# Short diagonal tiles of an attention pass: two or four heads in one PSUM bank and one exponential, with the written order rearranged

## The reference, cut to what matters

```python
scores = jnp.einsum('bhqd,bhkd->bhqk', Q, K)
causal = jnp.tril(jnp.ones((n, n), dtype=jnp.float32))
mask = (1.0 - causal) * -100000.0
attn = jax.nn.softmax((scores + mask) / math.sqrt(d), axis=-1)
out = jnp.einsum('bhqk,bhkd->bhqd', attn, V)
```

## Time and profile before

| | |
|---|---|
| median of 3 runs | 942.92 us (940.74 to 944.81) |
| the profiled execution, its own time | 941.0 us |
| its span, first to last instruction | 939.0 us |
| mean granted TensorE clock | 0.99 |
| PE busy | 900.1 us, 96% |
| VectorE (DVE) busy | 784.4 us, 84% |
| ScalarE (ACT) busy | 597.2 us, 64% |
| GpSimd (POOL) busy | 376.2 us, 40% |

### The profile page before, as it was taken

The page is one execution under the profiler, slowest core; times in us unless marked ns, Lnnn a source line. Parts: engine busy times, 40 slices in busy tenths (PEclk is TensorE's granted clock), DMA queues, the critical chain, the costliest instruction groups (busy, mean ns, idle before and its releaser), DMA issues.

```text
span 939.0 us, 17696 instructions
## 1 busy us (share of the span) xinstructions
PE 900.1 (96%) x5646; PEld 535.8 (57%) x5646; DVE 784.4 (84%) x2529; ACT 597.2 (64%) x1365; POOL 376.2 (40%) x526
## 2 busy tenths in 40 slices
PE   6788999899999999999999999999999999999996
PEld 5633355356665756456555656466565755555675
DVE  6889997998789799989889898998889998894543
ACT  3235676567766675776767675776767675776734
POOL 3713413323545335433364235534354224422434
PEclk9879999999999999999999999999999999999999
DMA  5311101200101011110021101110011011000000
GB/s 188 65 36 49 37 26 35 77 8 4 49 30 64 2 36 37 64 38 26 10 67 50 35 10 38 52 37 28 27 61 35 13 44 37 19 19 13 1 12 23
DMA packets 45980, 35.19 MB, mean 37 GB/s; under 512 B 10816, under 2 KB 44608, under 8 KB 45760
## 3 DMA queue, kind: packets, MB, share of 16 engines
q1 hardware_dynamic: 43680, 31.97, 10.7%
q10 hardware_dynamic: 2208, 2.10, 0.8%
HBM read 4.28 MB, written 4.19 MB: 9 GB/s over the span
## 4 chain that ended last, share of the span: by engine, by line
PE 84%; DVE 10%; ACT 2%; issue 2%; ACTq 1%; DMA 0%; SPq 0%; POOL 0%; POOLq 0%; DVEq 0%
PE bank_w L594 14%; PE bank_p L576 13%; PE bank_s L546 13%; PE bank_f L682 6%; PE bank_f L684 6%; PE bank_f L683 6%; PE bank_f L480 3%; PE bank_f L482 3%; PE bank_f L481 3%; PE bank_m L648 3%; DVE bank_s L784 3%; DVE mx_far L780 3%; PE bank_m L622 2%; PE bank_m L612 1%; PE bank_m L632 1%
## 5 line engine op out<-in xcount | busy, mean ns | idle before, releaser
L1051 ACT ACTIVATE pt<-bank_p 128x512 f32<-128x512 f32 (+3 forms) x768 | 350.0, 492 | 184.4 <-PE bank_p L576 160.2
L784 DVE CUSTOM_DVE_ANT_0 bank_s<-bank_s,causal 128x384 f32<-128x384 f32 (+3 forms) x512 | 244.7, 506 | 39.1 <-PE bank_s L546 35.9
L546 PE MATMUL bank_s<-k_stack,q_stack 96*128 96x512 bf16 (+3 forms) x768 | 236.0, 334 | 15.7 <-DVE mx L784 7.8
L576 PE MATMUL bank_p<-q_stack,k_stack 99*128 99x512 bf16 (+3 forms) x768 | 228.7, 332 | 4.1 <-ACT pt L1051 3.0
L780 DVE TENSOR_REDUCE mx_far<-bank_s 128x1 f32<-128x512 f32 x256 | 166.2, 683 | 21.5 <-PE bank_s L546 19.5
L1213 POOL TENSOR_SCALAR_AFFINE_SELECT pt<-pt 128x512 f32<-128x512 f32 x128 | 81.9, 641 | 221.5 <-ACT pt L1051 221.3
L594 PE MATMUL bank_w<-pt,v 128*32 128x512 f32 (+3 forms) x1536 | 154.9, 497 | 0.3 <-ACT ot L1042 0.2
L546 PEld LDWEIGHTS bank_s<-k_stack,q_stack 96*128 96x128 bf16 x768 | 72.3, 99 | 134.2 <-DVE mx L784 57.0
L576 PEld LDWEIGHTS bank_p<-q_stack,k_stack 99*128 99x128 bf16 x768 | 71.6, 99 | 113.2 <-ACT pt L1051 68.5
L682 PE MATMUL bank_f<-wex_h,hid_h 128*128 128x512 f32 x256 | 116.5, 455 | 0.8 <-DVE gate L936 0.7
L684 PE MATMUL bank_f<-wex_h,hid_l 128*128 128x512 f32 x256 | 101.3, 396 | 0.0
(11 more groups left out here) (139 smaller groups left out, 1417.8 us busy)
## 6 DMA issues: line engine op xcount, KB each, us to landing
q_stack<-qk_h SPq DMA_DIRECT2D x96, 64.0 KB, 2.6
k_stack<-qk_h SPq DMA_DIRECT2D x84, 64.0 KB, 2.6
q_stack<-qk_m SPq DMA_DIRECT2D x64, 64.0 KB, 2.6
out<-h SPq DMA_DIRECT2D x16, 256.0 KB, 2.5
k_stack<-qk_m SPq DMA_DIRECT2D x56, 64.0 KB, 2.6
q_stack<-qk_l SPq DMA_DIRECT2D x32, 64.0 KB, 2.6
k_stack<-qk_l SPq DMA_DIRECT2D x28, 64.0 KB, 2.4
x_sb<-x_t SPq DMA_DIRECT2D x16, 64.0 KB, 2.2
```

Source lines behind the costliest of these rows:

```text
L546: nc.tensor.matmul(s_bank[s % 2][:, 0:cols], q_stack[0:STACK, half, hd, t % HT * P:(t % HT + 1) * P], k_stack[0:STACK, hd, key_place(i, ha ...
L576: nc.tensor.matmul(p_bank[p % 2][:, q0:HALF], k_stack[:, hd, key_place(i, kt // HT), kt % HT * P:(kt % HT + 1) * P], q_stack[:, half, hd, ...
L784: nc.vector.tensor_tensor_reduce(src, src, causal[:, HALF - cols:HALF], 1.0, -3.0e38, ALU.add, ALU.max, mx[:, u, col:col + 1]).then_inc(s_ ...
L1051: nc.scalar.activation(pt[:, k % PT_SLOTS, j, q0:HALF], p_bank[p % 2][:, q0:HALF], ACT.Exp, scale=0.25).then_inc(exp_done, 1)
```

## The change

For a diagonal key tile with 256 columns two heads, and with 128 columns four heads, go side by side into one bank, and one exponential over all 512 columns of the bank follows. Full tiles and those of 384 columns stay as they were. The number of matmuls, their columns and their operands are the same; the first three of four (or the first of two) no longer signal. There are now 608 "p" items and exponentials in place of 768.

```diff
+def heads_a_bank(k):
+    return max(1, HALF // (HALF - first_column(k)))
+
+EXPS = [(k, j) for k in range(NP_) for j in range(0, G4, heads_a_bank(k))]
...
-                p = (i * NP_ + k) * G4 + j
+                p = i * NE_ + EXP_NO[k, j]
                 if p >= 2:
                     pe.wait_ge(exp_done, p - 1)
-                hd = g * G4 + j
-                nc.tensor.matmul(p_bank[p % 2][:, q0:HALF],
...
+                many, cols = heads_a_bank(k), HALF - q0
+                for m in range(many):
+                    hd = g * G4 + j + m
+                    to = m * cols if many > 1 else q0
+                    mm = nc.tensor.matmul(p_bank[p % 2][:, to:to + cols],
...
+                mm.then_inc(st_ready, 1)
...
+                    dst = pt[:, k % PT_SLOTS, j:j + many, q0:HALF]
+                    src = p_bank[p % 2][:].rearrange("p (j c) -> p j c", c=cols)
+                nc.scalar.activation(dst, src, ACT.Exp, scale=0.25).then_inc(exp_done, 1)
```

All waits on `st_ready` and `exp_done` count in the new items (`EXP_END[k]`). The five lists of `ORDER` are new. PE's has 2064 letters in place of 2224 and ScalarE's 982 in place of 1142, 160 "p" fewer each; the others keep their letters. Many items moved by one to three places, a few by up to 13. The first letters of three lists:

```diff
     "dve": (
-        "eaeiaaaaaaaaeasesssssssassssasssssasesstsssassassasssssssssassssssatssssasssssassssassassasssssassstssss"
...
+        "ieaeaaaaaaaaeasesssssssasssassssssasesstsssassassassssssssssasssssatssssasssssassssassassasssssassstssss"
...
     "act": (
-        "iaaaddfaaaddpppppppppppapppapppapppppppwppppppppwapppppppbppppappppppppppppppappppppbppppppppfppwppappff"
...
+        "iaaadfdaaaddppppppppapppapappppppppwppwapppppppbpppapppppppppppppppappbpppppppfppwppapffppppppffppppppfp"
...
     "sp": (
-        "eeidedddttdetdeddtdtdddtcdtddedtdctddtdctdddtedtddectedcdtdeddtddcdttddecteddddtdcdttdddtdcddttddectddet"
+        "eiededtddtdtdddtdtdddtecdteedddttdcddtdctdddtdtddcedtededtcdedtdtdcdtedcdtdddetdddctddtdtcdddetddtedtctd"
...
```

More of the change, by code:

```diff
@@ L71, in first_column @@
     return max(0, kt * P - UNITS[u][1] * HALF)
+def heads_a_bank(k):
+    return max(1, HALF // (HALF - first_column(k)))
+EXPS = [(k, j) for k in range(NP_) for j in range(0, G4, heads_a_bank(k))]
+EXP_NO = {e: n for n, e in enumerate(EXPS)}
+NE_ = len(EXPS)
+EXP_END = [sum(e[0] <= k for e in EXPS) for k in range(NP_)]
 FRONT_FILL = {"emb": 7, "turn1": 8, "q": 8, "k": 7, "v": 0}
@@ L104, in streams @@
         "s": scores,
-        "p": [("prob", k, j) for k in range(NP_) for j in range(G4)],
+        "p": [("prob", k, j) for k, j in EXPS],
         "w": weighing,
@@ L136, in works @@
         return (kind in ("stat1", "v", "stat2", "z2t", "hid", "combine", "constants", "forward_weights")
-                or (kind == "prob" and st[1] in DIAG and st[2] == G4 - 1))
+                or (kind == "prob" and st[1] in DIAG and st[2] == G4 - heads_a_bank(st[1])))
     return (kind in ("load", "turn", "queries", "rest")
@@ L149 @@
[L149 to L153, removed]
@@ new lines @@
+        "sswsstwspsasssswpssewspstpssppsppsspspspsbssppspssbssswssbwssbpwpwsppsappswsppbspswsbsfspspfptfppwpfspws"
+        "pfpspsafssfssfsppfssfssbwsbspfbsspfsspbsfssbspsftwsppwphspwsbpwspsbpspappfppfpfbwwppfepspfssppfpspwppwps"
+        "pfsspfpssapffsspapspfshpssfpsftswwwpsspfbspsfsbfssbpspsbsfafspwsswpspwwpspaspspwpspstpswepssbswswsppsasp"
+        "sffpsbpfafsspfppsswpfspfppfwspspbfbsfsppsbsfpbpsfbssfppshpwspspfbspswwssptfsspffssbspsfspspfspspfaspswpf"
+        "pswwspfptspwsspwsppfpssafpspsfsapspsfsppsasspfbfsshssfpsstpfpsspfssespfwwwwssapsswsppsassppsswspspssppsw"
@@ L435, in queries @@
                 if i:
-                    sp.wait_ge(st_ready, ((i - 1) * NP_ + UNIT_LAST[2 * half + g] + 1) * G4)
+                    sp.wait_ge(st_ready, (i - 1) * NE_ + EXP_END[UNIT_LAST[2 * half + g]])
                 for n in BY_PART_Q:
@@ L571, in prob @@
                     pe.wait_ge(other_keys_made, 1)
-                p = (i * NP_ + k) * G4 + j
+                p = i * NE_ + EXP_NO[k, j]
                 if p >= 2:
                     pe.wait_ge(exp_done, p - 1)
-                hd = g * G4 + j
-                nc.tensor.matmul(p_bank[p % 2][:, q0:HALF],
-                                 k_stack[:, hd, key_place(i, kt // HT), kt % HT * P:(kt % HT + 1) * P],
-                                 q_stack[:, half, hd, q0:HALF], start=True, stop=True).then_inc(st_ready, 1)
+                many, cols = heads_a_bank(k), HALF - q0
[3 more added lines that the diff above has]
+                    mm = nc.tensor.matmul(p_bank[p % 2][:, to:to + cols],
+                                          k_stack[:, hd, key_place(i, kt // HT), kt % HT * P:(kt % HT + 1) * P],
+                                          q_stack[:, half, hd, q0:HALF], start=True, stop=True)
+                mm.then_inc(st_ready, 1)
             def weigh(i, k):
@@ L584, in weigh @@
                 q0 = first_column(k)
-                pe.wait_ge(exp_done, (i * NP_ + k + 1) * G4)
+                pe.wait_ge(exp_done, i * NE_ + EXP_END[k])
                 if k in DIAG:
```

97 lines of the change are left out of this document (48 added, 49 removed).

## The result

The changed kernel took **945.28 us** (median of 20 runs, 943.94 to 948.38), the kernel before 943.00 (20 runs, 940.05 to 944.85). The ratio is **1.0028**, with a 95% interval from 1.0020 to 1.0037: 2.3 to 2.7 us slower, and clear of no change. The forecast was 940.5, a small gain. The time lies inside the forecast's range, its sign is wrong. The profiled execution of the kernel after took 946.43 us (span 944.7), that of before 941.0 (939.0).

A forecast was written before the change was run, and what follows sets the result against it. VectorE's reading of scores was taken to bound the start, PE's matmul stream the rest. Terms -0.7 - 2.8 + 0.7 + 1.5 = -1.3 us gave 939.7 (profiled) or 941.6 (median); forecast 940.5 us, the middle, range 930 to 949.

The forecast's parts named there:

- The cover is 1.0 us: Queries for score 32 would land at 52.2 us, ahead of its start at 53.25, so the later issue costs nothing.
- ScalarE and SP at the start: Start of the lists: feed-forward rounding ahead of group 1's keys, and maxima ahead of half 1's queries; both priced at 0.
- SP's move: SP's list at the start: maxima of unit 0 sent ahead of the twelve queries' DMAs of half 1; cost 0.
- ScalarE's work: Merged exponentials at 600 ns lower ScalarE from 597 to about 577 us; its share of the chain shrinks: -0.7 us.
- PE's work: The same 256 short matmuls, adjacent ones of 128 columns starting 0.06 us apart: cost 0, bounds -1 to +3 us.
- The waits for a bank: Second pass: short items' waits for an exponential to free a bank go, those of 384 columns stay: -2.8 us.
- VectorE at the start: `front_weights` moved to the front of VectorE's list makes `emb` start at 6.6, not 5.95, and `turn1` as late: +0.7 us.
- The moved items: Scores stand denser in PE's list; those without cover in images 1 to 7 go from 16.5 to 18.0 us: +1.5 us.
- rival C: Slower: denser scores make PE wait for VectorE to free banks, up to +10.1 us, 951 us; chance 0.18.
- Rival A: Larger gain: without the short items, waits of 384 and 512 column items go too; 933.2 us, chance 0.27.
- Rival B: Nothing: PE's stream is full and the waits that go were hidden; 941.0, or 942.9 in runs; chance 0.15.

The follow-up runs named there:

- s2_sp: Kernel after, with SP sending the maxima of unit 0 behind both groups of queries again, as before: 943.02 us, 1.0000 of the kernel before.
- b_sp: Kernel before, with only SP's maxima of unit 0 put ahead of the queries of half 1: 945.44 us, 1.0030 of the kernel before.
- y2_after_late: Kernel after, with GpSimd's 4.5 us subtraction held until VectorE has split the keys of half 1: 941.05 us, 0.9971 of the kernel before.
- y4_mid_late: Kernel after, with SP's maxima between the two query groups and GpSimd's subtraction held until the keys of half 1 are split: 939.39 us, 0.9953.
- s1_fw: Kernel after, with VectorE's `front_weights` back where it was: 945.45 us, 1.0031 of the kernel before.
- s4_clk: Kernel after, with fill matmuls added before 18 scores of image 1 to keep PE busier: 946.67 us, 1.0038 of the kernel before.
- x5_pe: Kernel after, with PE's list alone taken from before, each merged "p" at its first letter: 973.20 us, 1.0308 of the kernel before.
- s3_start: Kernel after, with the starts of the VectorE, SP and ScalarE lists all as before: 942.67 us, 1.0001 of the kernel before.

## Why the prediction was wrong

**The step that failed** is "The cover is 1.0 us" under ScalarE and SP at the start, which priced SP's move at 0. A mechanism was missing in it, two queues at work at once, and not only a size. It had the right queue, the right reader and the right warning ("without it each us is lost in full"), and three sizes wrong: the time of the maxima, the time of the issues, and the landing. It took the maxima as ready when they were in before; they came 1.5 us later (SP's first maxima issue at 45.57, so the queries could begin at 47.46, not 45.9). It took 3.7 us for six issues; two of them took 1.2 us longer, and the group ended at 52.44, not 49.6. And it took the median landing of 96 DMAs, 2.6 us, which the queries of half 1 had in before, where SP's queue was alone (2.4 to 2.6); with the keys' DMAs in the air the last query landed about 4.4 us after the end of its issue (52.44 to 56.8; the median counts from the start of an issue, so that adding it to the end was generous). 1.5 + 1.3 + 1.8 is 4.6 us; less the cover of 1.0, that is the +3.6 at which score 32 stands. Of these 1.5 are not SP's doing: they are at score 28 already, and in `s2_sp`, which loses nothing. The move alone is 2.0 us in the offsets at score 32, 2.3 in the medians of after and `s2_sp`, 2.5 in `b_sp`, 1.7 in `y2_after_late` against `y4_mid_late`. Score 32 waits for its queries in every kernel with the move (2.4, 1.5, 1.7, 1.6, 2.8 and 3.7 us in after, `s1_fw`, `s4_clk`, `b_sp`, `x5_pe` and `y2_after_late`) and in none without. Behind all of it is one thing: before, SP's queue was through with the queries when ScalarE's began the keys; the move makes SP wait, so that both load the DMA engines at once, and having the maxima sooner does not mend that (`y2_after_late`). The order alone would have fitted: begun at 47.46, with 3.7 us of issues and a landing of 2.6 us, the queries would have been there at 53.8, and score 32 ran at 54.8 in `s2_sp`. That is an estimate, and that the keys' queue is what stretches the landings is read from the tables; no kernel moved the keys.

**ScalarE's work**: right. 578.0 us against 577; the exponentials of 512 columns, 96 of them merged, take 598 ns in the mean against 600, so the gaps in the destination cost nothing that can be seen. (3.4% of 19 us is 0.6, not the 0.7 of the sum.) ScalarE's issues for the keys of group 1 ended at 27.8, ahead of the 29.5 forecast, and cost 0 as forecast.

**PE's work**: right at 0. PE stands idle 0.2 us in all before the matmuls of 128 columns, and where two of them follow each other in the kernel after (96 places) they start 55 to 60 ns apart but for a few, 58 ns in the mean: the 60 of my row held, not the 81 quoted beside it.

**The waits for a bank**: the mechanism was right, the term was not worth its 2.8 us. I counted, for 200 to 890 us, how much later each PE instruction starts than its pace allows. Matmuls of 128 columns lost 2.65 us before and 0.30 after, as forecast. But the total of all kinds went from 21.3 to 22.4 by this count, since full items (2.2 to 2.9), `bank_m` matmuls (1.3 to 3.2) and feed-forward matmuls (3.1 to 4.7) lost more. The times say the same: with SP's move taken out the change is worth 0.0 us (`s2_sp`, [-0.9, +0.9]), where my terms without it say -1.3. The step looked at each item's own wait alone and not at what follows it: the full items next to a bank that is now held twice as long explain 0.7 us at most, and what delays the `bank_m` and feed-forward matmuls stays open. The three kernels on old lists show that this is no small thing: there it is dearer than the gain. Which of the moved items repair it stays open: the new order without the merging was not tried.

**VectorE at the start**: `emb` came at 6.87, against 6.6 forecast and 5.95 before, and pushed `turn1` from 9.55 to 10.45:

```profile
6.06 0.36 DVE L979 CAST wqk_h<-z 128x128 fp32r<-128x128 f32 x2 [2.03 <-DMA bk_sb<-bk]
6.87 0.68 DVE L732 TENSOR_TENSOR h<-bank_m,pos_sb 128x512 f32<-128x512 f32 x1
10.45 0.86 DVE L750 TENSOR_SCALAR z<-h,mv,rs 128x128 f32<-128x128 f32 x3 [0.82 <-POOL rs L1207]
```

The size was within the bounds (+0.9), its worth was not: score 16 starts at 36.56 in both, and `s1_fw` regains nothing. I had taken an early delay as paid in full. But in both traces VectorE's cast ends with GpSimd's subtraction, and 0.8 us more or less ahead of it only makes the cast shorter or longer (4.15 us in after, 4.64 in `s1_fw`).

**The moved items and rival C**: 18.0 us without cover in my count against 16.5 before, but the excess ahead of 512-column scores between 200 and 890 us is 6.2 against 6.1. The weight loader's waits of scores for VectorE in the same stretch went from 50.0 to 51.4 us. The +1.5 did not show at the scores, and C, the denser scores, is false; the kernel is slower by another mechanism than the one that I had put on that side. **Rival A** is false: the loader waited 15 us less, and no time was gained by it. **Rival B**, nothing, describes the merging with its new lists well. That the measured time lay inside the range is luck: the range was wide for A and C, and neither came. The Trainium skill, Perfetto Trace Analysis, section Optimizing Scalar/DVE Operations, says that grouping can improve throughput if the engine is saturated; ScalarE was at 64%, nothing was gained, and so the runs agree (`s3_start` 1.0001).

## What to carry to other kernels

The landing time of a DMA in a profile holds for the traffic that it met there: before moving an issue, look at which other queue works in the new place, and don't take the old median for cover. Merging work of an engine that does not set the pace brought nothing here, and it holds the shared buffer longer for whoever comes next. Look for instructions whose duration differs from that of their own kind elsewhere: one cast of 2.66 us among others of 0.42 led to more than the whole change had promised, and one wait on an idle engine won it.

## What the runs showed of the hardware

**A VectorE instruction can stand until a whole GpSimd instruction has ended.** Cast and subtraction in before, then in after:

```profile
37.16 2.66 DVE L759 CAST qk_m<-qk_r 128x512 bf16<-128x512 f32 x1
35.03 4.50 POOL L1255 TENSOR_TENSOR wex_l<-hid,wex_h 128x2048 fp32r<-128x2048 f32 x1
```

```profile
37.17 4.15 DVE L771 CAST qk_m<-qk_r 128x512 bf16<-128x512 f32 x1
36.53 4.51 POOL L1272 TENSOR_TENSOR wex_l<-hid,wex_h 128x2048 fp32r<-128x2048 f32 x1
```

The cast ends 0.29 us after the subtraction (39.53 and 39.82, 41.04 and 41.32), and so in `s1_fw` and `s3_start`, however late it began; GpSimd's subtraction keeps its 4.5 us in every trace. It hits a VectorE cast or subtraction whose operands are all in SBUF, even one of 16 x 128 elements (`mrow_l` above); readings of PSUM (0.33) and a subtraction with one operand in PSUM (0.28) beside the same GpSimd instruction keep their length. The Trainium skill, SBUF — State Buffer, section Terms, says that the two share one pair of ports, and that the one without it is blocked for a full instruction. These rows agree for VectorE; none shows GpSimd held for the length of a VectorE instruction.

**Two DMA queues at once** moved 113 to 135 GB/s over 5 us in blocks of 64 KB, with a share of packet times of 0.94 to 1.18 (the lowest rate in `b_sp`, 55 to 60 us, at a share of 1.00; the highest in `y2_after_late`, 45 to 50 us, at 1.09), where one queue alone moved 101, its own pace of issuing, at a share of 0.29. The second queue added at most a third to the rate, and the median landings rose from between 2.4 and 2.6 us to between 4.0 and 6.5.
